# Block-diagonal keys against 64-row products in the attention scores of one stage of a four-layer kernel

## The chip, the cores and the metric

The kernel runs on one NeuronCore of a Trainium2 chip. The metric is the device time of one execution in microseconds (us). The times shown are medians of several executions, and a profile is one further execution taken by the hardware profiler.

## What is computed

The reference is a residual stack over x of shape 2 x 1024 x 256: in each of four layers a cross-attention block and a feed-forward block, each on the layer-normed x. The change lies in the feed-forward block of layer 0, here called L0 ffn, which is itself a small transformer: two layers of windowed local attention with a gated feed-forward. Cut to what matters:

```python
for l in range(2):                       # DEPTH
    q, k, v = split(shift_token(x) @ wqkv[l])      # 8 heads of 64
    q, k = rotary_xpos(l2norm(q) * qs, l2norm(k) * ksc)
    # windows of 128 queries, each on its own and the preceding window: 256 keys
    sim = einsum('bhwid,bhwjd->bhwij', bq * 8.0, bk)
    attn = softmax(where(mask, -big, sim))
    x = x + (attn @ bv) @ wo[l]
    h = layernorm(shift_token(x)) * g + b
    x = x + gated_gelu(h @ w1 + b1) @ w2 + b2
```

A head has 64 dimensions, so a score of one head is a product over 64 rows of the array of TensorE, which has 128 rows. Everything here is float32, apart from the mask, which is added to the scores as a bfloat16 product with the identity.

## The kernel before, in words

`l0_ffn` works through 32 items: two layers, eight tiles of 128 positions and two batches; four items (two tiles, two batches) make one turn of a hardware loop (`layers`, L896 and on). An item has its number `q` in the turn, its batch `b` (which picks one of two halves of the PSUM, banks 0 to 3 or 4 to 7), and `odd`, which says in which half of the key window its own keys stand. The work is a software pipeline written out by hand: `step(now, new, after)` is run on each engine, and in one step `now` goes from its probabilities to its output, `new` from its projections to its probabilities, and `after` has its input transposed. Each engine runs its list in order and waits for semaphores of the others. There is no planner.

TensorE's list in a step, in order: half of a projection of `new` (L977), `mixed(now)` (L1015, probabilities times values), projections of `new` between `mix_transposed` (L1023), `attention_out` (L1029) and `shifted` (L1035, L1036) of `now`, `h2_transposed` (L1042), `ffn_up` (L1052), `qk_transposed(new)` (L987), `y_transposed(after)` (L968), `ffn_down` of the first four of six chunks (L1061), then **scores(new)** (L998 and L999), the transposes of the probabilities of bank 0 (L1006), the last two chunks of `ffn_down` (L1061; the very last chunk has only 42 rows), and the transposes of banks 1 to 3 (L1006).

In `scores` one PSUM bank holds the scores of two heads, 2 x 256 columns. For each of four banks TensorE adds the mask (one product of 512 bfloat16 columns, L998) and then multiplies the 128 rows of queries of two heads by 128 rows of keys (512 columns, L999). So that two heads don't mix, the keys are block-diagonal: `kT` has for each pair of heads the keys of the one in rows 0 to 63 of the first 256 columns, those of the other in rows 64 to 127 of the last 256, and zeros elsewhere, which GpSimd writes once at the start (L839). A float32 product is carried out in two passes, so each of these is two MATMUL records with a load of weights (LDWEIGHTS) before each.

Around it: ScalarE copies the queries (`copy_qT`, L1140), VectorE the keys in two copies of 64 partitions (`copy_kT`, L1276). VectorE then takes, for each bank as it gets ready, the maximum of each row and head (`maxima`, L1286) and the bias of the exponential (L1287). ScalarE computes the exponentials of eight heads with their sums (`probs`, L1146), two per bank, as each bias gets ready. TensorE transposes the probabilities bank by bank (L1006); ScalarE copies banks 0 and 1 of the transposes (L1155) and VectorE banks 2 and 3 (`copy_pT`, L1293), and `mixed` waits for both. `mix` (L1297, L1300) divides by the sums.

Of the kernel before, what the change touches and what calls it, by code (L numbers as in the profile page):

```python
# [7 lines left out]
ALU = mybir.AluOpType  # L8
# [7 lines left out]
P = 128  # L16
BATCH, SEQ, D = 2, 1024, 256
# [48 lines left out]
def memory(e, ctx, stage):  # L66

    return lambda name, shape, dt=F32: ctx.enter_context(e.nc.sbuf_tensor(f"{stage}_{name}", shape, dt))


def flat(ap):
    return ap.rearrange("p a b -> p (a b)")
# [99 lines left out]
def build(nc, dram, out):  # L172
    with ExitStack() as ctx:
# [36 lines left out]
        with ExitStack() as early:  # L210
            ffn = L0Ffn(e, early)
            with ExitStack() as earlier:
                x1 = L0Xattn(e, earlier)
                prologue(e, x1)
                l0_xattn(e, x1, ffn)
            l0_ffn(e, ffn)
# [558 lines left out]
HEADS, DH = 8, 64  # L775
# [6 lines left out]
HALF = TILES // 2  # L782


def l0_ffn(e, ffn):

    nc, s, d, ps = e.nc, e.s, e.dram, e.psum
    dve, act, pool = (e.chain[n] for n in ("dve", "act", "pool"))  # L790
    with ExitStack() as ctx:
        sb = memory(e, ctx, "l0_ffn")
# [6 lines left out]
        mask_even = sb("mask_even", [P, HALF, 2 * P], BF16)  # L799
        mask_odd = sb("mask_odd", [P, 2 * P], BF16)  # L800
# [5 lines left out]
        pT = sb("pT", [P, BATCH, 2 * HEADS, P])  # L806
        ss = sb("ss", [P, BATCH, 2 * HEADS])
        rn = sb("rn", [P, BATCH, 2 * HEADS])
        qT = sb("qT", [P, BATCH, 4, P])
        kT = sb("kT", [P, BATCH, 4, 2, 2, P])  # L810
        vv = sb("vv", [P, BATCH, 2, INNER])
        top = sb("att_top", [P, BATCH, HEADS])
        scale = sb("att_scale", [P, BATCH, HEADS])
        bias = sb("att_bias", [P, BATCH, HEADS])
        den = sb("att_den", [P, BATCH, HEADS])
        rden = sb("att_rden", [P, BATCH, HEADS])
        o = sb("o", [P, BATCH, INNER])
        oT = sb("oT", [P, BATCH, 4, P])
        y1 = sb("y1", [P, BATCH, 2, D])
# [88 lines left out]
        with nc.Block() as block:  # L908
# [52 lines left out]
            def _(pe):  # L961
# [29 lines left out]
                def scores(m):  # L991
                    pe.wait_ge(s.v_ready.sem, s.v_ready.at(m.turn, m.k))
                    pe.wait_ge(s.qT_ready.sem, s.qT_ready.at(m.turn, m.k))
                    pe.wait_ge(s.kT_ready.sem, s.kT_ready.at(m.turn, m.k))
                    for j in range(4):
                        bank = ps[:, m.bank + j, :]
                        mask = (mask_odd[:].unsqueeze(1) if m.odd else mask_even[:, bass.ds(m.i, 1), :]).broadcast_to((P, 2, 2 * P))
                        pe.matmul(bank, e.ident_bf[:], mask, start=True, stop=False)  # L998
                        pe.matmul(bank, qT[:, m.b, j, :], kT[:, m.b, j, :, :, :].rearrange("p h w n -> p (h w n)"),  # L999
                                  start=False, stop=True).then_inc(s.scores_psum.sem, 1)  # L1000

                def probs_transposed(m, banks):
                    for j in banks:
# [6 lines left out]
                def mixed(m):  # L1010
                    pe.wait_ge(s.pT_act.sem, s.pT_act.at(m.turn, 2 * m.k))
                    pe.wait_ge(s.pT_dve.sem, s.pT_dve.at(m.turn, 2 * m.k))
                    for h in range(HEADS):
                        for c in range(2):
                            mm = pe.matmul(ps[:, m.bank, h * DH:(h + 1) * DH], pT[:, m.b, 2 * h + c, :],  # L1015
                                           vv[:, m.b, c, h * DH:(h + 1) * DH], start=(h, c) == (0, 0), stop=c == 1,
                                           skip_group_check=True)
                    mm.then_inc(s.mixed_psum.sem, 1)
# [48 lines left out]
                def first(new, after):  # L1067
                    y_transposed(new)
                    for n in range(3):
                        qkv(new, n)  # L1070
                    qk_transposed(new)
                    y_transposed(after)
                    scores(new)
                    probs_transposed(new, range(4))

                def step(now, new, after):
                    if new:
                        qkv(new, 0, (0,))
                    mixed(now)
                    if new:  # L1080
                        qkv(new, 0, (1,))
                    mix_transposed(now)
                    if new:
                        qkv(new, 1, (0,))
                    attention_out(now)
                    if new:
                        qkv(new, 1, (1,))
                    shifted(now)
                    if new:
                        qkv(new, 2)  # L1090
                    h2_transposed(now)
                    ffn_up(now)
                    if new:
                        qk_transposed(new)
                    if after:
                        y_transposed(after)
                    ffn_down(now, 0)
                    ffn_down(now, 1)
                    if new:
                        scores(new)  # L1100
                        probs_transposed(new, (0,))
                    ffn_down(now, 2)
                    if new:
                        probs_transposed(new, (1, 2, 3))
# [109 lines left out]
            def _(v):  # L1214
# [56 lines left out]
                def copy_kT(m):  # L1271
                    v.wait_ge(s.qkT_psum.sem, s.qkT_psum.at(m.turn, m.k))
                    v.wait_ge(s.scores_psum.sem, s.scores_psum.at(m.turn, 4 * (m.k - 2)))
                    for n in range(2):
                        own = slice(n * DH, (n + 1) * DH)
                        cp = v.tensor_copy(kT[own, m.b, :, n, m.odd, :], ps[own, m.bank + 1, :].rearrange("p (j n) -> p j n", j=4))  # L1276
                    cp.then_inc(s.kT_ready.sem, 1)

                def maxima(m):
                    v.wait_ge(s.q_norm_ready.sem, s.q_norm_ready.at(m.turn, m.k))  # L1280
                    v.wait_ge(s.probs_ready.sem, s.probs_ready.at(m.turn, 4 * (m.k - 2)))
                    v.tensor_scalar(scale[:, m.b, :], rn[:, m.b, 0:HEADS], float(DH) ** 0.5, None, ALU.mult)
                    for j in range(4):
                        v.wait_ge(s.scores_psum.sem, s.scores_psum.at(m.turn, 4 * (m.k - 1) + j + 1))
                        heads = slice(2 * j, 2 * j + 2)
                        dve.link(v.tensor_reduce(top[:, m.b, heads], ps[:, m.bank + j, :].rearrange("p (n x) -> p n x", n=2), AX.X, ALU.max))  # L1286
                        v.scalar_tensor_tensor(bias[:, m.b, heads], top[:, m.b, heads], -1.0, scale[:, m.b, heads],  # L1287
                                               ALU.mult, ALU.mult).then_inc(s.bias_ready.sem, 1)
# [5 lines left out]

                def mix(m):
                    v.wait_ge(s.probs_ready.sem, s.probs_ready.at(m.turn, 4 * m.k))
                    dve.link(v.reciprocal(rden[:, m.b, :], den[:, m.b, :]))  # L1297
                    v.wait_ge(s.mixed_psum.sem, s.mixed_psum.at(m.turn, m.k))
                    v.wait_ge(s.mixT_psum.sem, s.mixT_psum.at(m.turn, m.k - 2))
                    v.tensor_tensor(o[:, m.b, :].rearrange("p (h x) -> p h x", x=DH), ps[:, m.bank, :].rearrange("p (h x) -> p h x", x=DH),  # L1300
                                    rden[:, m.b, :].unsqueeze(2).broadcast_to((P, HEADS, DH)), ALU.mult).then_inc(s.mix_ready.sem, 1)

                def add_attention(m):
                    v.wait_ge(s.out_psum.sem, s.out_psum.at(m.turn, m.k))
# [45 lines left out]
                def first(new, after):  # L1350
                    take_y(new)
                    take_y(after)
                    tables(new.layer)
                    norms(new)
                    rotate_cos(new)
                    rotate_sin(new)
                    rotate_sum(new)
                    scale_k(new)
                    copy_kT(new)
                    maxima(new)  # L1360
# [1622 lines left out]
```

## Time and profile before

| what | value |
|---|---|
| median of 3 executions | 2155.83 us (2154.03 to 2156.53) |
| span of the profiled execution | 2156.2 us |
| TensorE matmuls busy | 1694.4 us (79%) |
| VectorE busy | 1111.4 us (52%) |
| ScalarE busy | 758.4 us (35%) |
| GpSimd busy | 438.6 us (20%) |
| L0 ffn, from its first scores to its last | 199.6 to about 1145 us of the span |

The profiled execution is one execution and its own time is its span, from its first to its last instruction. Shares are averages over stages that differ much: what a change in L0 ffn is worth is read from the stretch 199.6 to 1145 us alone. In the rows PE is a matmul, PEld a load of weights, DVE VectorE, ACT ScalarE, POOL GpSimd, and L followed by a number is the line of the kernel. The record of a matmul is longer than the time for which it keeps the next one waiting: starts are read from the records, ends are modelled.

### The profile page before, as it was taken

The numbers are of one execution on the slowest core, as the hardware profiler recorded it, in microseconds if no ns is written. First come the engines' busy times: TensorE is split into PE (matmuls) and PEld (weight loads), VectorE is DVE, ScalarE is ACT, GpSimd is POOL, SyncE is SP. The second block draws the span as 40 slices with busy tenths as digits, with TensorE's granted clock in tenths as the row PEclk, the third lists the DMA queues.
The fourth block names the chain that finished last, engine by engine and source line by source line (L and its number), as shares of the span: only waits on it lengthen the run. The fifth ranks groups of instructions, "written<-read, shape, count | busy, mean of one in ns | idle before, by whom it ended". The sixth has DMA issues, their size and how long they took to land. (4 is left out here: it accounts for less than half of the span.)

```text
span 2156.2 us, 31922 instructions
## 1 busy us (share of the span) xinstructions
PE 1694.4 (79%) x9560; PEld 1268.2 (59%) x9561; DVE 1111.4 (52%) x2565; ACT 758.4 (35%) x1808; POOL 438.6 (20%) x451
## 2 busy tenths in 40 slices
PE   5965999999999999999997839629824479847990
PEld 4653666666666666666666629528713147636990
DVE  3335555556555655565554650157666856562212
ACT  1211544445444444444443213204426223312330
POOL 1012111111111221222211122241131500007005
PEclk9977999999999999999997559869957589958995
DMA  5001000000001000000000212151000000014114
GB/s 199 0 0 46 1 1 0 0 0 0 0 1 46 1 1 0 0 0 0 0 1 29 88 63 66 56 195 56 3 27 0 0 3 0 0 40 115 34 36 122
DMA packets 30065, 66.49 MB, mean 31 GB/s; under 512 B 6438, under 2 KB 21815, under 8 KB 28460
## 3 DMA queue, kind: packets, MB, share of 16 engines
q1 hardware_dynamic: 23900, 48.99, 6.3%
q0 software_dynamic: 6096, 16.65, 2.9%
q8 instruction: 34, 0.56, 0.1%
q14 instruction: 35, 0.29, 0.0%
HBM read 51.04 MB, written 14.59 MB: 30 GB/s over the span
## 5 line engine op out<-in xcount | busy, mean ns | idle before, releaser
L1052 PE MATMUL banks<-l_ffn_h2T,l_ffn_w 128*128 128x128 f32 (+1 forms) x1536 | 185.0, 279 | 32.2 <-ACT l_ffn_h2T L1166 32.2
L1052 PEld LDWEIGHTS banks<-l_ffn_h2T,l_ffn_w 128*128 128x128 f32 (+1 forms) x1536 | 173.8, 182 | 42.9 <-issue 39.0
L977 PE MATMUL banks<-l_ffn_in_wqkv,l_ffn_hT 128*128 128x512 f32 x384 | 197.2, 611 | 1.9 <-issue 1.1
L1146 ACT ACTIVATE l_ffn_work<-banks,l_ffn_att_bias,l_ffn_att_scale 128x256 f32<-128x256 f32 x256 | 140.6, 568 | 51.8 <-DVE l_ffn_att_bias L1287 51.8
L942 POOL TENSOR_TENSOR l_ffn_rstd<-l_ffn_ve,neg_half 128x1 f32<-128x1 f32 x32 | 17.8, 557 | 658.2 <-DVE l_ffn_ve L1315 658.2
L1015 PEld LDWEIGHTS banks<-l_ffn_vv,l_ffn_pT 128*128 128x128 f32 x1024 | 119.3, 195 | 33.3 <-ACT l_ffn_pT L1155 29.6
L999 PE MATMUL banks<-l_ffn_kT,l_ffn_qT 128*128 128x512 f32 x256 | 132.8, 601 | 0.0
L1015 PE MATMUL banks<-l_ffn_vv,l_ffn_pT 128*128 128x64 f32 x1024 | 122.7, 279 | 8.8 <-DVE l_ffn_pT L1293 5.1
L1286 DVE TENSOR_REDUCE l_ffn_att_top<-banks 128x2 f32<-128x512 f32 x128 | 88.5, 692 | 62.3 <-PE banks L999 62.3
L256 POOL TENSOR_TENSOR rstd<-mean_var,neg_half 128x1 f32 (+1 forms) x80 | 46.0, 576 | 346.9 <-DVE mean_var L249 346.7
L1176 ACT ACTIVATE l_ffn_gate<-banks,l_ffn_layer_cols 128x128 f32<-128x128 f32 x192 | 59.8, 362 | 136.5 <-PE banks L1052 136.5
L2035 POOL DMA_INDIRECT l_experts_rows<-l_experts_y_rows,l_experts_back x64 | 62.4, 975 | 211.7 <-DMA l_experts_y_rows<-l_experts_y 192.8
L1061 PE MATMUL banks<-l_ffn_in_w,l_ffn_ff 128*128 128x256 f32 (+1 forms) x384 | 99.6, 388 | 0.0
L1160 ACT COPY l_ffn_oT<-banks 128x512 f32<-128x512 f32 x32 | 18.8, 586 | 202.1 <-PE banks L1023 202.1
L1300 DVE TENSOR_TENSOR l_ffn_o<-banks,l_ffn_att_rden 128x512 f32<-128x512 f32 x32 | 22.1, 692 | 130.6 <-PE banks L1015 99.6
L1899 POOL DMA_INDIRECT l_experts_rows<-l_experts_c_rows,l_experts_token x63 | 62.0, 984 | 128.3 <-POOLq L1795 109.7
L1183 ACT ACT_TABLE_LOAD x63 | 80.8, 1283 | 1.1
L1995 DVE COPY l_route_c_all<-l_ffn_in_w 128x1024 f32 x39 | 27.6, 709 | 103.4 <-PE banks L1928 90.7
L1928 PEld LDWEIGHTS banks<-l_experts_rowT,l_route_c_all 128*128 128x128 f32 x624 | 78.1, 197 | 1.9
L977 PEld LDWEIGHTS banks<-l_ffn_in_wqkv,l_ffn_hT 128*128 128x128 f32 x384 | 64.7, 195 | 24.0 <-issue 21.2
L1928 PE MATMUL banks<-l_experts_rowT,l_route_c_all 128*128 128x128 f32 x624 | 78.3, 281 | 0.0
L932 POOL TENSOR_TENSOR l_ffn_rn<-l_ffn_ss,neg_half 128x8 f32<-128x8 f32 x32 | 52.7, 1646 | 118.5 <-DVE l_ffn_ss L1247 118.5
(377 smaller groups left out, 3700.8 us busy)
## 6 DMA issues: line engine op xcount, KB each, us to landing
l_ffn_in_w<-in_L_w SPq DMA_DIRECT2D x2, 4096.0 KB, 20.2
l_experts_y_rows<-l_experts_y SPq DMA_DIRECT2D x63, 128.0 KB, 1.7
l_ffn_in_down<-in_L_down SPq DMA_DIRECT2D x1, 4096.0 KB, 13.0
l_experts_c_rows<-l_route_c_all SPq DMA_DIRECT2D x2, 2048.0 KB, 8.5
l_ffn_in_wqkv<-in_L_wqkv SPq DMA_DIRECT2D x1, 3072.0 KB, 12.8
l_ffn_w<-in_L_w SPq DMA_DIRECT2D x2, 1364.0 KB, 7.0
x_res<-in_x SPq DMA_DIRECT2D x4, 512.0 KB, 5.5
l_ffn_rot<-in_rotary SPq DMA_DIRECT2D x2, 1024.0 KB, 4.8
```

Of the source, the lines that this page charges most:

```text
L977: mm = pe.matmul(ps[:, m.bank + 1 + n, :], hT[:, m.b, m.odd, ch, 1 - ch:P + 1 - ch], wqkv[:, bass.ds(m.layer, 1), ch, n * INNER:(n + 1) * ...
L999: pe.matmul(bank, qT[:, m.b, j, :], kT[:, m.b, j, :, :, :].rearrange("p h w n -> p (h w n)"), start=False, stop=True).then_inc(s.scores_ps ...
L1015: mm = pe.matmul(ps[:, m.bank, h * DH:(h + 1) * DH], pT[:, m.b, 2 * h + c, :], vv[:, m.b, c, h * DH:(h + 1) * DH], start=(h, c) == (0, 0), ...
L1052: mm = pe.matmul(ps[0:FW[j], m.bank + j // 2, to:to + P], w1[:, ch, at:at + FW[j]], h2T[:, ch, m.b, :], start=(j % 2, n, ch) == (0, 0, 0), ...
L1061: mm = pe.matmul(ps[:, m.bank + 3, 0:D], ff[0:FW[j], j, :], w2[0:FW[j], bass.ds(m.layer, 1), j, :].rearrange("p l n -> p (l n)"), start=j ...
L1146: ex = nc.scalar.activation(work[:, m.b, slot, :], ps[:, m.bank + slot // 2, (slot % 2) * 2 * P:(slot % 2 + 1) * 2 * P], ACT.Exp, bias=bia ...
L1176: g = nc.scalar.activation(gate[0:FW[j], j, :], ps[0:FW[j], m.bank + j // 2, of:of + P], ACT.Gelu, bias=cols[0:FW[j], col:col + 1])
L1183: act.link(nc.scalar.activation(unused[:], zero, func))
L1286: dve.link(v.tensor_reduce(top[:, m.b, heads], ps[:, m.bank + j, :].rearrange("p (n x) -> p n x", n=2), AX.X, ALU.max))
L1899: p.indirect_dma_start(rows[:, t, :], None, c_rows, bass.IndirectOffsetOnAxis(ap=token[:, t:t + 1], axis=0))\
L1928: mm = pe.matmul(ps[m.j][:, f * P:(f + 1) * P], w, rowT[:, m.j, ch, :], start=(f, ch) == (0, 0), stop=ch == DCH - 1, skip_group_check=True)
L2035: p.indirect_dma_start(rows[:, i, :], None, y_rows, bass.IndirectOffsetOnAxis(ap=back[:, i:i + 1], axis=0))\
```

## The change

The keys are stored densely (`kT` has half the size, one copy of 128 partitions instead of two of 64), and each head becomes a product over 64 rows: heads with even numbers in rows 0 to 63, odd ones in rows 64 to 127, 256 columns each. Two heads that follow each other in the list use different row halves and write different banks. So that this is so, the order of heads in the banks changes (`slot_of`): a group `g` of four heads is held in two banks, bank `2g` with the two heads of the lower row half, bank `2g+1` with the two of the upper. In each group TensorE first adds the masks to both banks, and then issues four products: lower, upper, lower, upper. Banks `2g` and `2g+1` are both signalled near the end of their group. `scale`, the reciprocal of the sums and the products of `mixed` read and write in the changed order.

```diff
+def slot_of(head):
+    return head // 4 * 4 + head % 2 * 2 + head // 2 % 2
+def in_slots(ap):
+    return ap.rearrange("p (g n a) -> p g a n", g=2, n=2)
+def in_heads(ap):
+    return ap.rearrange("p (g a n) -> p g a n", g=2, n=2)
...
-        kT = sb("kT", [P, BATCH, 4, 2, 2, P])
+        kT = sb("kT", [P, BATCH, 4, 2, P])
...
-                    for j in range(4):
-                        bank = ps[:, m.bank + j, :]
-                        mask = (...)
-                        pe.matmul(bank, e.ident_bf[:], mask, start=True, stop=False)
-                        pe.matmul(bank, qT[:, m.b, j, :], kT[:, m.b, j, :, :, :].rearrange("p h w n -> p (h w n)"),
-                                  start=False, stop=True).then_inc(s.scores_psum.sem, 1)
+                    mask = (...)
+                    for g in range(2):
+                        for n in range(2):
+                            pe.matmul(ps[:, m.bank + 2 * g + n, :], e.ident_bf[:], mask, start=True, stop=True)
+                        for half in range(2):
+                            for n in range(2):
+                                own, j = slice(n * DH, (n + 1) * DH), 2 * g + half
+                                mm = pe.matmul(ps[:, m.bank + 2 * g + n, half * 2 * P:(half + 1) * 2 * P], qT[own, m.b, j, :],
+                                               flat(kT[own, m.b, j, :, :]), start=False, stop=True, skip_group_check=True)
+                                if half == 1:
+                                    mm.then_inc(s.scores_psum.sem, 1)
...
-                            mm = pe.matmul(ps[:, m.bank, h * DH:(h + 1) * DH], pT[:, m.b, 2 * h + c, :],
+                            mm = pe.matmul(ps[:, m.bank, h * DH:(h + 1) * DH], pT[:, m.b, 2 * slot_of(h) + c, :],
...
-                    for n in range(2):
-                        own = slice(n * DH, (n + 1) * DH)
-                        cp = v.tensor_copy(kT[own, m.b, :, n, m.odd, :], ps[own, m.bank + 1, :].rearrange("p (j n) -> p j n", j=4))
-                    cp.then_inc(s.kT_ready.sem, 1)
+                    v.tensor_copy(kT[:, m.b, :, m.odd, :], ps[:, m.bank + 1, :].rearrange("p (j n) -> p j n", j=4))\
+                     .then_inc(s.kT_ready.sem, 1)
...
-                    v.tensor_scalar(scale[:, m.b, :], rn[:, m.b, 0:HEADS], float(DH) ** 0.5, None, ALU.mult)
+                    v.tensor_scalar(in_slots(scale[:, m.b, :]), in_heads(rn[:, m.b, 0:HEADS]), float(DH) ** 0.5, None, ALU.mult)
...
-                    dve.link(v.reciprocal(rden[:, m.b, :], den[:, m.b, :]))
+                    dve.link(v.reciprocal(in_heads(rden_h[:, m.b, :]), in_slots(den[:, m.b, :])))
```

## Rows read from the trace of the kernel before

**Rows 1.** Two stretches: length, busy us of PE, PEld, DVE, ACT, POOL, granted clock, DMA.

```profile
199.50:681.00 481.50, 455.04 (x2554) 321.56 (x2555) 275.28 (x597) 225.38 (x578) 81.75 (x64) 0.99 0.01 3
...
719.00:1141.00 422.00, 396.84 (x2238) 281.01 (x2237) 249.59 (x573) 198.43 (x503) 89.12 (x84) 1.00 0.00 0
```

**Rows 2.** Timeline of TensorE over one step (start, us, instructions, idle before).

```profile
746.67 1.89 PE L1061 MATMUL banks<-l_ffn_in_w,l_ffn_ff 128*128 128x256 f32 x8
748.40 0.38 PE L998 MATMUL banks<-l_ffn_mask_odd,ident_bf 128*128 128x512 bf16 x1
748.62 1.02 PE L999 MATMUL banks<-l_ffn_kT,l_ffn_qT 128*128 128x512 f32 x2
...
752.70 0.60 PE L1006 MATMUL banks<-ident,l_ffn_work 128*128 128x128 f32 x4
...
754.29 1.56 PE L1006 MATMUL banks<-ident,l_ffn_work 128*128 128x128 f32 x12
755.69 1.02 PE L977 MATMUL banks<-l_ffn_in_wqkv,l_ffn_hT 128*128 128x512 f32 x2
756.85 3.76 PE L1015 MATMUL banks<-l_ffn_vv,l_ffn_pT 128*128 128x64 f32 x32
...
768.42 0.44 PE L1042 MATMUL banks<-ident,l_ffn_h 128*128 128x128 f32 x2 [0.45 <-DVE l_ffn_h L1321]
```

**Rows 3.** Timeline of VectorE in the same step.

```profile
749.68 0.69 DVE L1286 TENSOR_REDUCE l_ffn_att_top<-banks 128x2 f32<-128x512 f32 x1 [1.29 <-PE banks L999]
...
755.42 1.29 DVE L1293 COPY l_ffn_pT<-banks 128x512 f32<-128x512 f32 x2 [0.47 <-PE banks L1006]
```

**Rows 4.** Timeline of ScalarE in the same step.

```profile
750.66 0.56 ACT L1146 ACTIVATE l_ffn_work<-banks,l_ffn_att_bias,l_ffn_att_scale 128x256 f32<-128x256 f32 x1 [1.49 <-DVE l_ffn_att_bias L1287]
...
751.76 0.56 ACT L1146 ACTIVATE l_ffn_work<-banks,l_ffn_att_bias,l_ffn_att_scale 128x256 f32<-128x256 f32 x1
...
754.92 0.22 ACT L1146 ACTIVATION_READ_ACCUMULATOR l_ffn_work<-banks,l_ffn_att_bias,l_ffn_att_scale 128x1 f32 x1
```

**Rows 5.** Timeline from 128-row to 42-row chunks of L1061, in short windows.

```profile
753.14 0.60 PE L1061 MATMUL banks<-l_ffn_in_w,l_ffn_ff 128*128 128x256 f32 x2
...
753.66 0.70 PE L1061 MATMUL banks<-l_ffn_in_w,l_ffn_ff 42*128 42x256 f32 x2
...
754.29 0.20 PEld L1006 LDWEIGHTS banks<-ident,l_ffn_work 128*128 128x128 f32 x2 [0.33 <-ACT l_ffn_work L1146]
```

**Rows 6.** Timeline of two 64-row products in different row halves, L535, in growing windows.

```profile
63.71 0.48 PE L535 MATMUL banks<-ctx_tok,l_xattn_aT 64*128 64x256 f32 x1
...
63.71 0.49 PE L535 MATMUL banks<-ctx_tok,l_xattn_aT 64*128 64x256 f32 x2
...
63.71 0.70 PE L535 MATMUL banks<-ctx_tok,l_xattn_aT 64*128 64x256 f32 x4
```

**Rows 7.** Groups of VectorE's PSUM copies by form (count, busy us, mean ns, idle before).

```profile
L1276 DVE COPY l_ffn_kT<-banks 64x512 f32<-64x512 f32 x64 | 43.7, 683 | 2.5 <-PE banks L987 2.1
L1293 DVE COPY l_ffn_pT<-banks 128x512 f32<-128x512 f32 x64 | 41.2, 686 | 16.5 <-PE banks L1006 14.5 <-issue 1.3 <-DVE l_ffn_y L1227 0.7
```

**Rows 8.** Timelines at other steps: first, layer change, two behind a loop's branch.

```profile
199.55 0.59 PE L998 MATMUL banks<-l_ffn_mask_even,ident_bf 128*128 128x512 bf16 x1 [1.15 <-DVE l_ffn_kT L1276]
...
690.95 1.07 ACT L1155 COPY l_ffn_pT<-banks 128x512 f32<-128x512 f32 x2 [0.61 <-ACT l_ffn_layer_b L1115]
...
718.45 0.39 PE L998 MATMUL banks<-l_ffn_mask_even,ident_bf 128*128 x1
...
720.65 0.56 ACT L1146 ACTIVATE l_ffn_work<-banks,l_ffn_att_bias,l_ffn_att_scale 128x256 f32<-128x256 f32 x1 [1.55 <-DVE l_ffn_att_bias L1287]
...
814.45 0.42 DVE L1338 TENSOR_TENSOR x_res<-banks,l_ffn_y1b 128x256 f32 x1 [0.70 <-PE banks L1061]
...
816.52 1.29 DVE L1293 COPY l_ffn_pT<-banks 128x512 f32<-128x512 f32 x2 [0.54 <-issue]
```

**Rows 9.** Timeline of GpSimd and VectorE in the preparation of the stage.

```profile
169.46 3.51 POOL L839 MEMSET l_ffn_kT<- 128x4096 f32 x1 [0.31 <-POOLq L741]
172.91 1.95 POOL L840 MEMSET l_ffn_vv<- 128x2048 f32 x1
...
169.50 10.02 DVE L845 TENSOR_SCALAR l_ffn_y<-x_res,mean_var,rstd 128x256 f32<-128x256 f32 x16 [1.18 <-PEq L741]
```

More of the change, by code:

```diff
@@ L815, in l0_ffn @@
         den = sb("att_den", [P, BATCH, HEADS])
-        rden = sb("att_rden", [P, BATCH, HEADS])
+        rden_h = sb("att_rden", [P, BATCH, HEADS])
         o = sb("o", [P, BATCH, INNER])
@@ L994, in scores @@
                     pe.wait_ge(s.kT_ready.sem, s.kT_ready.at(m.turn, m.k))
-                    for j in range(4):
-                        bank = ps[:, m.bank + j, :]
-                        mask = (mask_odd[:].unsqueeze(1) if m.odd else mask_even[:, bass.ds(m.i, 1), :]).broadcast_to((P, 2, 2 * P))
-                        pe.matmul(bank, e.ident_bf[:], mask, start=True, stop=False)
-                        pe.matmul(bank, qT[:, m.b, j, :], kT[:, m.b, j, :, :, :].rearrange("p h w n -> p (h w n)"),
-                                  start=False, stop=True).then_inc(s.scores_psum.sem, 1)
+                    mask = (mask_odd[:].unsqueeze(1) if m.odd else mask_even[:, bass.ds(m.i, 1), :]).broadcast_to((P, 2, 2 * P))
+                    for g in range(2):
[8 more added lines that the diff above has]
+                                    mm.then_inc(s.scores_psum.sem, 1)
                 def probs_transposed(m, banks):
@@ L1300, in mix @@
                     v.tensor_tensor(o[:, m.b, :].rearrange("p (h x) -> p h x", x=DH), ps[:, m.bank, :].rearrange("p (h x) -> p h x", x=DH),
-                                    rden[:, m.b, :].unsqueeze(2).broadcast_to((P, HEADS, DH)), ALU.mult).then_inc(s.mix_ready.sem, 1)
+                                    rden_h[:, m.b, :].unsqueeze(2).broadcast_to((P, HEADS, DH)), ALU.mult).then_inc(s.mix_ready.sem, 1)
                 def add_attention(m):
```

## The prediction

> **What bounds the kernel now.** I read the busy times by stretch first. In L0 ffn TensorE's matmul records cover 852 of 903.5 us at a granted clock of 0.99 to 1.00, the 2.4 GHz level, and no other engine covers 60% [rows 1]. That looks like a stage in which every matmul saved is time saved. But records overlap, so I read one step's timeline next, TensorE first and then the engines that it meets around the scores.
>
> The step's scores start at 748.40 and the next work of TensorE, the transposes, at 752.70: 4.30 us for four banks, each a mask of 0.22 us and a product of two passes of 0.43 us (748.40 to 748.62, then 1.02 less the 0.59 of a record) [rows 2]. Next to it runs a second chain: bank 0 ready, VectorE's maximum at 749.68 (1.28 after the start of the scores), ScalarE's first exponential at 750.66, its last sum at 755.14, the last transposes, VectorE's second copy, and `mixed` at 756.85 [rows 2 to 4]. The eight exponentials go at 1.10 us for two (750.66 to 751.76) without a gap; they take 4.48 us in all [rows 4]. **Both chains arrive together.** TensorE's own work puts bank 3's transposes at about 755.2, and the last exponentials allow them at that time too; their record ends at 755.85 [rows 2]. VectorE copies two banks from 755.42, 1.29 us of which the second starts at 756.03 (1.29 less the 0.68 of one copy, [rows 3, 7]). So the second copy would bear bank 3 some 0.13 us later than it comes (756.03, against 755.85 and the 0.05 from a record's end to VectorE's start). After `mixed` all of TensorE's work follows in order, and what it waits for there (0.45 us at L1042, [rows 2]) hangs on `mixed` itself. **A step is therefore longer or shorter by what `mixed` moves against the start of the scores.**
>
> **The change, part by part.**
>
> *TensorE's work in the scores.* A group is now two masks (2 x 0.215 = 0.43), then 64-row products, 256 columns each. A pass of 256 float32 columns takes 0.215 us (0.60 less 0.38 for two of L1061) [rows 5]. Two 64-row products in different row halves run at once: L535 has four passes; the first alone has a record of 0.48 us, the first of both end 0.49 after the start, and all four are over in 0.70, where four passes in a row would need 0.48 + 3 x 0.215 = 1.1 [rows 6]. So a group's eight passes take four times 0.215 = 0.86. The price is the change of rows in use. After a 128-row pass that starts at 753.36 and streams to 753.57, the 42-row ones start at 753.66, and the second of them at 753.98 (753.66 + 0.70 - 0.38), so the first streams from 753.77: **0.20 us** in which nothing streams [rows 5]. Going back costs some 0.14 (0.09 to the load of weights at 754.29, and part of the load). A group: 0.43 + 0.20 + 0.86 + 0.14 = 1.63, a step's scores 3.26 instead of 4.30, 1.04 us less for TensorE.
>
> The Trainium skill, "TensorEngine Tiling (Array Packing)", section Theoretical Speedup, gives up to 2x for a contraction of 64 rows or fewer. By that figure alone the products' 3.42 us a step would halve, and 32 steps would save about 55 us; the trace agrees with the doubling in a pair, and against the rest stand the 0.34 us a group for the switches.
>
> *When the banks get ready.* Bank 0 was complete 0.22 + 0.86 = 1.08 after the start. Now it needs both masks, the switch and both of its heads: 0.43 + 0.20 + 0.86 = 1.49. **It is 0.41 us later**, while banks 1 to 3 are earlier (bank 1 1.49 for 2.15, bank 2 3.1 for 3.2, bank 3 3.1 for 4.3). VectorE needs about 0.89 us a bank, ScalarE 1.10, so only bank 0 sets the pace of the exponentials, and they all end 0.41 later: 755.55 for 755.14. Bank 3's transposes follow them; TensorE has nothing else to issue in between. Bank 3 is ready at 755.85 + 0.41 + 0.05 = 756.31, and VectorE, free at 756.03, waits 0.28. `mixed` is 0.28 us later. TensorE's gained 1.04 us is spent in waits before the transposes. In 9 of these steps, those behind a loop's branch, the exponentials start 2.20 after the scores (718.45 to 720.65, [rows 8]) and not 2.26, and it is 0.22. **27 like steps x 0.26 = +7.0 us.**
>
> *The steps that differ.* At the layer change ScalarE itself is last before `mixed` (its own copies follow the exponentials directly) [rows 8]: +0.4. At three ends of a turn in the second layer VectorE's copies come late, 816.52, behind statistics that wait for `ffn_down`, 814.45 [rows 8]. That product follows bank 0's transposes, which wait for two exponentials: 750.66 + 0.41 + 1.10 + 0.2 = 752.3 instead of 752.70. So it is 0.37 earlier: 3 x 0.37 = **-1.1**. In the first step the scores do wait for the keys' copy, 1.15 us [rows 8]: one copy of 128 partitions takes 0.69 like L1293's, for 1.37 with two [rows 7]: **-0.7**. I take its slower banks (half clock) as even, since its exponentials had gaps to fill.
>
> *The keys' copy elsewhere* frees 0.69 us of VectorE a step, 22 us in all, and I cost it at nothing: TensorE starts the scores 0.22 after the last pass of its own `ffn_down` (746.67 + 1.89 - 0.38 = 748.18, [rows 2]), at once, and VectorE then waits 1.29 us for bank 0 [rows 3]. If the copy were on the path it would give up to 0.1 a step.
>
> *The zeros.* GpSimd writes 4096 columns in 3.51 us, and VectorE's sixteen operations of that stretch stand still under it; the stage starts when they are done. 2048 columns take 1.95 [rows 9]: **-1.6**. The reordered views of 8 elements and the changed index in `mixed` change no count or size: nothing.
>
> **Sum:** 7.0 + 0.4 - 1.1 - 0.7 - 1.6 = **+4.0 us** on the profiled 2156.2, whose span is 0.4 above the median of 2155.83: 2159.8, or +0.18%. About 0.2%, 4.3 us, is what a measurement of this kernel can tell from no change.
>
> **Bounds of the unknown term**, the switch to 64 rows right behind a bfloat16 mask, which no row shows. With no cost, bank 0 is 0.21 late and the slack takes most of it: 27 x 0.06 + 0.2 - 3.4 = -1.6, 2154.2. At twice 0.20, a load and a gap not overlapping, 0.61 late: 27 x 0.46 + 0.6 - 0.9 - 2.3 = +9.8, 2165.6. I take 0.20, the nearest row.
>
> **Rivals.**
>
> *The products don't run together (slower).* Rows 6 show two products behind a wait; here four follow without one, and the load for the third could hold up the fourth. If the passes go one by one, bank 0 needs 0.43 + 0.20 + 6 x 0.215 = 1.92, 0.84 late, and a group costs TensorE 2.48, 4.96 a step for 4.30. `mixed` is 0.70 later in 27 steps: +18.9 + 0.8 + 2.0 (three ends) - 2.3 = +19.4, **2175**. It decides from the third pass on: bank 0 over 1.6 us after the start. Chance 9%. That two heads gain nothing at all from the halves is the same case: the change then doesn't do what it says.
>
> *TensorE's saving comes through (faster).* If `mixed` follows TensorE's list and not the exponentials, a step loses 1.04 us: 32 x 1.04 + 2.3 = 35.6, **2120**. For it speaks the full TensorE of rows 1. Against it: TensorE has only the transposes, two chunks and half a projection between scores and `mixed`, and the exponentials' 4.48 us can't start before bank 0. The skill, same page, section PSUM Bottleneck, says that tiling speeds up TensorE but not the reading of PSUM; the trace agrees, with 4.48 us of exponentials beside 3.26 of scores. Chance 9%.
>
> *The longer waits lower the clock.* TensorE would idle about 1.3 us a step more, in pieces under 0.6. With waits of such size the stretch holds 1.00 [rows 1, 2]. A few us, chance 4%.
>
> **Numbers.** The forecast with its bounds has 78%: of it 3% of all is faster by over 0.2%, 43% within, 32% slower. With the rivals: faster 12%, same 44%, slower 44%. The range is 2153.5 to 2166, the bounds with the runs' spread; the two rivals lie outside.
>
> **What would show it.** Pairs of L999 starts 0.01 apart, four starts 0.215 apart, behind a gap of 0.1 and a record longer by 0.1 (concurrency, switch). The first maximum 1.69 after the first mask for 1.28. ScalarE's exponentials still gapless. Waits of TensorE's loads in L1006 on ScalarE, new, some 1 us a step. `mixed` 8.7 us after the first mask for 8.45. GpSimd's first write at 1.95. A `mixed` less than 8.3 after the first mask would prove the forecast wrong, a first maximum after 1.9 the serial rival right.

## The result and the profile after

The changed kernel takes 2175.3 us (median of 4, 2174.60 to 2175.83), against 2155.18 for the kernel before (4 executions): a ratio of 1.0095, interval 1.0081 to 1.0109. It is 20 us slower, where the forecast had it 4 us slower and the range ended at 2166. The number 2175 stood in the prediction beside the serial rival. That is a coincidence: the trace shows another cause.

The page of the profile of the changed kernel: its span, busy times, granted clock by slices and the two queues that bring instructions:

```profile
span 2173.8 us, 32402 instructions
## 1 busy us (share of the span) xinstructions
PE 1678.0 (77%) x9816; PEld 1266.6 (58%) x9817; DVE 1080.3 (50%) x2533; ACT 757.5 (35%) x1808; POOL 436.0 (20%) x451
...
PEclk9977999999999999999998559959958579958995
...
q8 instruction: 35, 0.57, 0.1%
q14 instruction: 45, 0.37, 0.1%
```

TensorE is busy 16 us less than before and VectorE 31 us less, and the span is 17.6 us longer. The queue q14 carries 45 packets; it carried 35 in the kernel before.

TensorE in the step that answers to [rows 2] (start, us, instructions, idle before):

```profile
747.67 1.89 PE L1079 MATMUL banks<-l_ffn_in_w,l_ffn_ff 128*128 128x256 f32 x8
749.40 0.59 PE L1011 MATMUL banks<-l_ffn_mask_odd,ident_bf 128*128 128x512 bf16 x2
749.92 1.14 PE L1015 MATMUL banks<-l_ffn_kT,l_ffn_qT 64*128 64x256 f32 x8
750.99 0.61 PE L1011 MATMUL banks<-l_ffn_mask_odd,ident_bf 128*128 128x512 bf16 x2
751.52 1.13 PE L1015 MATMUL banks<-l_ffn_kT,l_ffn_qT 64*128 64x256 f32 x8
753.32 0.65 PE L1024 MATMUL banks<-ident,l_ffn_work 128*128 128x128 f32 x4 [0.66 <-ACT l_ffn_work L1164]
...
756.60 0.66 PE L1024 MATMUL banks<-ident,l_ffn_work 128*128 128x128 f32 x4 [0.44 <-ACT l_ffn_work L1164]
...
758.13 3.76 PE L1033 MATMUL banks<-l_ffn_vv,l_ffn_pT 128*128 128x64 f32 x32
```

The same place in two shorter windows, of which the first ends after one product's record and the second after two:

```profile
749.61 0.38 PE L1011 MATMUL banks<-l_ffn_mask_odd,ident_bf 128*128 128x512 bf16 x1
749.92 0.48 PE L1015 MATMUL banks<-l_ffn_kT,l_ffn_qT 64*128 64x256 f32 x1
...
749.92 0.49 PE L1015 MATMUL banks<-l_ffn_kT,l_ffn_qT 64*128 64x256 f32 x2
```

Here the forecast holds nearly to the hundredth. Two passes of a group are over in 0.49 us and all eight in 1.14, which is 0.49 and three more times 0.215: they run two at a time. A group repeats after 750.99 - 749.40 = 1.59 (forecast 1.63). New waits on ScalarE, 0.66 and 0.44 us, stand before the transposes, and `mixed` starts 8.73 after the first mask (forecast 8.7, before 8.45, [rows 2]).

VectorE and ScalarE in the same step, for [rows 3, 4]:

```profile
751.09 0.69 DVE L1302 TENSOR_REDUCE l_ffn_att_top<-banks 128x2 f32<-128x512 f32 x1 [2.54 <-PE banks L1015]
...
757.29 0.69 DVE L1309 COPY l_ffn_pT<-banks 128x512 f32<-128x512 f32 x1 [0.40 <-PE banks L1024]
```

```profile
752.07 0.56 ACT L1164 ACTIVATE l_ffn_work<-banks,l_ffn_att_bias,l_ffn_att_scale 128x256 f32<-128x256 f32 x1 [1.90 <-DVE l_ffn_att_bias L1303]
```

The first maximum is 1.69 after the first mask, as forecast, where it was 1.28. The like steps cost what was forecast for them. **Most of the time went elsewhere, at the ends of the turns in the second layer.** This is the end of the first of them, which answers to 814.45 and 816.52 in [rows 8], first on VectorE and then on TensorE:

```profile
815.57 0.42 DVE L1354 TENSOR_TENSOR x_res<-banks,l_ffn_y1b 128x256 f32 x1 [0.66 <-PE banks L1079]
...
816.95 0.16 DVE L1364 TENSOR_TENSOR mean_var<-mv,zero_eps 128x2 f32 x1
820.22 1.29 DVE L1309 COPY l_ffn_pT<-banks 128x512 f32<-128x512 f32 x2 [3.11 <-issue]
```

```profile
817.69 1.12 PE L990 MATMUL banks<-l_ffn_in_wqkv,l_ffn_hT 128*128 128x512 f32 x2
821.65 5.39 PE L1033 MATMUL banks<-l_ffn_vv,l_ffn_pT 128*128 128x64 f32 x32 [2.84 <-DVE l_ffn_pT L1309]
```

VectorE waits 3.11 us for nothing that the profile knows ("issue"), where it waited 0.54 [rows 8]. That is the place at which its loop goes back to its start. TensorE waits 2.84 us for VectorE, and then 32 passes take 5.39 us in place of 3.76. The busy times around it (start and end, length, PE, PEld, DVE, ACT, POOL, granted clock, DMA):

```profile
815.00:823.50 8.50, 5.19 (x33) 3.47 (x32) 2.65 (x8) 2.91 (x10) 0.56 (x1) 1.00 0.01 4
823.50:830.30 6.80, 6.80 (x25) 5.15 (x24) 0.69 (x1) 0.48 (x1) 0.00 (x0) 0.50 0.00 0
830.30:846.00 15.70, 14.20 (x87) 11.06 (x86) 10.33 (x23) 7.19 (x17) 5.80 (x5) 1.00 0.00 0
```

From 823.5 on the granted clock is 0.50, the 1.2 GHz level, for 6.8 us. The same stands at the second turn's end, with waits of 3.04 and 2.72 us. The last turn's end is another matter: VectorE has no such wait there, but the clock fell to 0.50 too, from about 1076 to 1083, behind waits of TensorE of 0.60, 0.44 and 0.79 us.

### The profile page after: what moved, and what is told of

It reads as the page before. It is cut to its first block and busy times, and to the rows that moved or that the text cites. A ratio compares the mean times of both kernels' runs of the same rounds, so it can differ in the third digit from the quotient of the medians.

```text
span 2173.8 us, 32402 instructions
## 1 busy us (share of the span) xinstructions
PE 1678.0 (77%) x9816; PEld 1266.6 (58%) x9817; DVE 1080.3 (50%) x2533; ACT 757.5 (35%) x1808; POOL 436.0 (20%) x451
## 5 line engine op out<-in xcount | busy, mean ns | idle before, releaser
L1033 PEld LDWEIGHTS banks<-l_ffn_vv,l_ffn_pT 128*128 128x128 f32 x1024 | 125.7, 204 | 32.8 <-ACT l_ffn_pT L1173 25.1
L1033 PE MATMUL banks<-l_ffn_vv,l_ffn_pT 128*128 128x64 f32 x1024 | 129.1, 288 | 8.7 <-DVE l_ffn_pT L1309 6.4
L1024 PE MATMUL banks<-ident,l_ffn_work 128*128 128x128 f32 x512 | 80.2, 287 | 34.9 <-ACT l_ffn_work L1164 34.9
L1079 PE MATMUL banks<-l_ffn_in_w,l_ffn_ff 128*128 128x256 f32 (+1 forms) x384 | 99.6, 388 | 0.0
L1024 PEld LDWEIGHTS banks<-ident,l_ffn_work 128*128 128x128 f32 x512 | 53.7, 141 | 69.8 <-ACT l_ffn_work L1164 55.3
```

Source lines behind the costliest of these rows:

```text
L1024: mm = pe.transpose(ps[:, m.bank + j, n * P:(n + 1) * P], work[:, m.b, 2 * j + n // 2, (n % 2) * P:(n % 2 + 1) * P], e.ident[:])
L1079: mm = pe.matmul(ps[:, m.bank + 3, 0:D], ff[0:FW[j], j, :], w2[0:FW[j], bass.ds(m.layer, 1), j, :].rearrange("p l n -> p (l n)"), start=j ...
```

## The experiments

Two theories. **A, placement:** the change removes one VectorE instruction of each step's list (the second copy of the keys), nine of them ahead of the second layer's loop. All later code of VectorE moves forward by nine instructions and the loop's body shrinks from 278 to 274. It now lies so that its return has to wait for instructions from memory. **B, the scores:** TensorE's new waits bring the clock down, and the long turns are a consequence. The experiments ran in two sets on two chips, on both of which the kernel before is slower than in the result; the second set is the change again, the heads in another order, and the scores moved in the kernel before. The kernel before takes 2206.85 us (21 executions) with the first set and 2208.49 (15) with the second, 2.4% more. Like steps of L0 ffn are as long on all of them to a few hundredths. From the last scores to the end it is 1061 to 1070 us there and 1015 in the trace of the kernel before, so the difference lies behind this stage. Ratios and differences are taken within a set unless it is said.

### Nine instructions put back

```diff
                     tables(new.layer)
+                    for n in range(9):
+                        v.memset(ff[:, 0, n:n + 1], 0.0)
```

> The changed kernel with nine one-column memsets put into VectorE's list once, where VectorE waits for the first squares, so that all its later code stands nine instructions further on, as before the change. Theory A (placement: the second layer's loop body of VectorE, 274 instructions, has come to lie over one more 8 KB piece of code, and its return waits 2.9 us for instructions): the branch's wait is back at about 0.3 us in each of the turns, the clock stays at 1.00 through the second layer, and the time is about 2160 (2158 to 2162), 15 us less than the change's 2175.3. Theory B (the scores: the new waits of TensorE before the transposes bring the clock down, and the long turns are its consequence): nothing moves, 2175. In both the first maximum stands 1.69 us after the first mask and mixed 8.73 after it.

2210.28 us (11 executions), ratio to the kernel before 1.0016 (1.0007 to 1.0025), which is 3.4 us more (1.5 to 5.5). The turn's end, the instruction queue, and the stretch of the second layer:

```profile
814.22 0.16 DVE L1364 TENSOR_TENSOR mean_var<-mv,zero_eps 128x2 f32 x1
814.92 1.29 DVE L1309 COPY l_ffn_pT<-banks 128x512 f32<-128x512 f32 x2 [0.54 <-issue]
```

```profile
q14 instruction: 35, 0.29, 0.0%
```

```profile
749.00:1140.00 391.00, 356.42 (x2167) 255.55 (x2166) 219.26 (x518) 182.90 (x466) 82.71 (x78) 1.00 0.00 0
```

The wait at the return is gone, ten packets of instructions are gone, and the clock is 1.00 throughout, with all of TensorE's new waits before the transposes still there. Theory B falls for the two returns. Nine writes of one column took away most of the loss, which the next run measures in these conditions. What is left, 3.4 us, agrees with the forecast's 4.0.

### The change again, in the second set

> The changed kernel itself, on the chip of the experiments, for a direct comparison with the nine memsets (3.4 us above the kernel before there). Theory A: some 14 to 17 us more than with them, about 17 to 20 us above the kernel before, ratio 1.008 to 1.009.

2223.43 us (5 executions), 1.0073 (1.0058 to 1.0088): 15 us above the kernel before. It is 13.0 above the run of the same set that has the nine writes and the heads in another order, and by the differences to the kernel before, 14.9 and 3.4, it is 11.5 above the nine writes alone: a little under what was expected. In this execution two turns' ends have the wait (3.00 in the row below) and half a clock behind it. The last turn's end has the same waits of TensorE as in the result (0.61, 0.44 and 0.78 us) and the full clock, and its step is 3.1 us shorter than there. So that part differs between executions of one kernel, and its cause stays open.

```profile
818.20 1.29 DVE L1309 COPY l_ffn_pT<-banks 128x512 f32<-128x512 f32 x2 [3.00 <-issue]
```

### The keys copied twice

```diff
-                    v.tensor_copy(kT[:, m.b, :, m.odd, :], ps[:, m.bank + 1, :].rearrange("p (j n) -> p j n", j=4))\
-                     .then_inc(s.kT_ready.sem, 1)
+                    for n in range(2):
+                        own = slice(n * DH, (n + 1) * DH)
+                        cp = v.tensor_copy(kT[own, m.b, :, m.odd, :], ps[own, m.bank + 1, :].rearrange("p (j n) -> p j n", j=4))
+                    cp.then_inc(s.kT_ready.sem, 1)
```

> The changed kernel with the keys copied in two copies of 64 partitions, as before, into the dense keys; the products are those of the change. VectorE's loop bodies then have as many instructions as before the change, 256 and 278, and stand where they stood. Theory A: no long wait at the return, about 2160.5 (0.7 us more than with the nine memsets, from the first step, where the copy is on the path). Theory B: 2175 or more, since TensorE's list is the change's. If the keys' copy were on the path in every step: 0.69 us x 31 = 21 us more than with the nine memsets.

2212.06 us (10 executions), 1.0034 (1.0019 to 1.0050). No long wait, 35 packets on q14: the placement is restored without any filler. It is 1.8 us above the nine writes where 0.7 was expected, and far from the 21 that the copy would cost on the path. The first mask of the stage:

```profile
195.92 1.01 PE L1011 MATMUL banks<-l_ffn_mask_even,ident_bf 128*128 128x512 bf16 x2 [1.15 <-DVE l_ffn_kT L1294]
```

It waits 1.15 us for the keys, where it waits 0.45 with the nine writes: the 0.70 of the first step, as forecast. The other steps, the layer change left aside, are together 1.35 us longer than with the nine writes, most of it at ends of turns, so the second copy accounts for about 2 us. The times themselves are less sharp than that: six executions lie between 2210.7 and 2212.2 and four between 2215.5 and 2222.3, for a reason that no trace here shows. In the profiled execution the layer change ran at the full clock and its step took 32.58 us for 37.09 with the nine writes, one more place where the clock differs between executions.

### The kernel before, moved by 115 instructions

```diff
                     tables(new.layer)
+                    for n in range(115):
+                        v.memset(ff[:, 0, n:n + 1], 0.0)
```

> The kernel before with 115 one-column memsets put into VectorE's list once, in its wait for the first squares (some 7 us of work in a wait of 6 us, so at most 2 us of cost by themselves). Theory A: its loop of the second layer, 278 instructions, starts 115 further on and lies over one more piece of 128 instructions: a wait of about 2.9 us at two returns, half a clock for about 7 us behind them, and 2155.2 + 12 to 16 = about 2169 (2165 to 2173). Theory B, or any in which the products matter: at most 2157.

2219.69 us, 1.0058 (1.0043 to 1.0073): 12.8 us slower, as theory A had it, with no change to any product or copy.

```profile
816.10 0.16 DVE L1348 TENSOR_TENSOR mean_var<-mv,zero_eps 128x2 f32 x1
819.41 1.29 DVE L1293 COPY l_ffn_pT<-banks 128x512 f32<-128x512 f32 x2 [3.15 <-issue]
```

```profile
q14 instruction: 46, 0.38, 0.1%
```

```profile
819.50:829.70 10.20, 8.85 (x35) 7.69 (x36) 2.00 (x4) 0.00 (x0) 0.00 (x0) 0.50 0.00 2
```

The steps at these two ends take 38.04 and 38.43 us for 31.29 and 31.30 in the kernel before, 13.9 more together, which accounts for the whole loss. Their waits of TensorE are longer than in the changed kernel (3.67 and 3.55 us), and so is the half clock behind them, 10.2 us for 6.8. Wait, packets and half clock are all made by place alone. The number 115 was chosen on the assumption that instructions are held in pieces of 128: a shift by 115 forward then puts the body where a shift by 13 backward would, close to the 9 backward of the change. It bore out, but other numbers were not tried, so the length of a piece is supported and not shown.

The Trainium skill, "Runtime: NRT & Kernel Launch", section Instruction fetch mechanics, says that an engine's instruction memory is filled in sequence and that a taken branch to a place outside it waits for a fetch; this case's traces agree on the branch, and give the price at a loop's return: 3.1 us for 0.54. The same section has blocks of 16 KiB; the packets of q14 here hold 8 KB each (0.37 MB in 45). Whether one or two of them make a block no run here shows directly. That 9 backward and 115 forward both bring the wait speaks for one, if 128 instructions fill a packet: the two places lie 124 instructions apart.

### Heads in another order

```diff
-                        for half in range(2):
-                            for n in range(2):
+                        for n in range(2):
+                            for half in range(2):
```

This run has the nine writes too.

> The changed kernel with the nine memsets, and with the products of a group in the order lower, lower, upper, upper in place of lower, upper, lower, upper. If the array takes products of the other row half only as they come up in the list, the two halves overlap in part or not at all: bank 1 gets ready up to 0.86 us later, a group costs TensorE 2.0 to 2.5 us for 1.6. Bank 0 is ready as before, 1.69 after the first mask with VectorE's start. By the forecast's mechanism partial overlap (groups of 2.0) costs nothing, since TensorE has 0.66 us of waits before the first transposes: as the nine memsets, within 3 us. With no overlap at all TensorE's list becomes the bound: mixed about 9.1 after the first mask, +0.4 us x 31 = 12 us.

2210.46 us (10 executions), 1.0007 (0.9997 to 1.0017): 2.0 us above the kernel before, as with the nine writes within the noise. The products did not lose their overlap at all:

```profile
748.58 0.49 PE L1015 MATMUL banks<-l_ffn_kT,l_ffn_qT 64*128 64x256 f32 x2
...
748.58 1.14 PE L1015 MATMUL banks<-l_ffn_kT,l_ffn_qT 64*128 64x256 f32 x8
749.65 0.60 PE L1011 MATMUL banks<-l_ffn_mask_odd,ident_bf 128*128 128x512 bf16 x2
```

Eight passes in 1.14 us again, though the first four in the list use the lower rows and the last four the upper. One after the other, the eight would need 0.48 + 7 x 0.215 = 2.0, and the first two, which are over in 0.49 (the first row, from a short window), would need 0.70. So in this list the products of the upper half did not wait for those of the lower half ahead of them. The serial rival and the partly serial one are both out.

### Scores ahead of a part of ffn_down

```diff
                     ffn_down(now, 0)
-                    ffn_down(now, 1)
                     if new:
                         scores(new)
+                    ffn_down(now, 1)
+                    if new:
                         probs_transposed(new, (0,))
```

This was run once in the changed kernel with the nine writes, and once in the kernel before.

> The changed kernel with the nine memsets, and with the scores of the next item moved ahead of the second pair of chunks of ffn_down (0.86 us of TensorE's work). By the forecast's mechanism (mixed hangs on bank 0, not on TensorE's list) the scores start up to 0.8 us earlier, which the keys' copy now allows (it ends 0.92 us before the first mask, in the kernel before 0.21), and the 0.86 us go into the wait before the transposes: about 0.75 us less in each of 31 steps, 2160 - 23 = about 2137 (2130 to 2143), faster than the kernel before. If TensorE's own list set the step, the order would change nothing: 2160.

In the changed kernel: 2191.72 us (4 executions, 2186.73 to 2195.49), ratio to the kernel before 0.9924 (0.9908 to 0.9939), 18.6 us less than with the nine writes (expected: 23) and **15 us less than the kernel before**. TensorE, where the first masks now follow four passes of L1079 and the other four stand behind the scores:

```profile
737.63 1.03 PE L1079 MATMUL banks<-l_ffn_in_w,l_ffn_ff 128*128 128x256 f32 x4
738.59 0.59 PE L1011 MATMUL banks<-l_ffn_mask_odd,ident_bf 128*128 128x512 bf16 x2
...
741.78 1.13 PE L1079 MATMUL banks<-l_ffn_in_w,l_ffn_ff 128*128 128x256 f32 x4
742.75 0.60 PE L1024 MATMUL banks<-ident,l_ffn_work 128*128 128x128 f32 x4
...
745.79 0.66 PE L1024 MATMUL banks<-ident,l_ffn_work 128*128 128x128 f32 x4 [0.36 <-ACT l_ffn_work L1165]
747.33 3.76 PE L1033 MATMUL banks<-l_ffn_vv,l_ffn_pT 128*128 128x64 f32 x32
```

The wait of 0.66 before the first transposes is filled, and `mixed` is again 8.74 after the first mask, though 0.86 us more of TensorE's work lies between them. A step is 29.46 us (738.59 to 768.05) for 30.23 (749.40 to 779.63): 0.77 less, as expected. From the first mask of the stage to the last the two profiled executions take 924.9 us and, with the nine writes, 946.6: 21.7 less. The first mask comes 5.0 later here (199.25 for 194.22): 3.4 of that stand before the first work of TensorE in this stage, in code that the move doesn't touch, and 1.6 come from a longer stretch at the slow clock in the first projections.

> The kernel before with the scores of the next item moved ahead of the second pair of chunks of ffn_down. There the copies of the keys end only 0.21 us before the first mask and TensorE has no waits in the scores' neighbourhood to fill, so that the move alone should bring little: the first mask can come at most 0.1 us earlier, and ffn_down's 0.86 us then stand in TensorE's way before the transposes: 0 to 0.1 us a step, within 4 us of the kernel before. If it gains as much as in the changed kernel (20 us against its base), the dense keys have no part in that gain.

In the kernel before the same move costs time: 2234.48 us (4 executions), 1.0123 (1.0105 to 1.0140), 26 us more. The expectation of at most 4 us was wrong.

```profile
758.90 1.03 PE L1061 MATMUL banks<-l_ffn_in_w,l_ffn_ff 128*128 128x256 f32 x4
760.56 0.38 PE L998 MATMUL banks<-l_ffn_mask_odd,ident_bf 128*128 128x512 bf16 x1 [0.63 <-DVE l_ffn_kT L1277]
...
764.85 1.03 PE L1061 MATMUL banks<-l_ffn_in_w,l_ffn_ff 128*128 128x256 f32 x4
...
769.87 3.76 PE L1015 MATMUL banks<-l_ffn_vv,l_ffn_pT 128*128 128x64 f32 x32 [0.18 <-DVE l_ffn_pT L1294]
```

The first mask waits 0.63 for the keys' second copy, and `mixed` comes 9.31 after it instead of 8.45: TensorE's list is full there, so the moved 0.86 us is paid in full after the scores, and with the wait before them almost nothing of it comes back: a step takes 30.75 us for 29.95. The expectation had named both and set them off against each other. By these rows the gain of the move needs both things that the dense keys bring, the shorter list of TensorE and the earlier copy; a kernel with only one of them was not run with the move.

## Why the prediction was wrong

- **The groups and the overlap: right.** 1.59 us a group for 1.63; two row halves at once, the switch to 64 rows at 0.20: the first pair starts at 749.92, 0.31 after the second mask, with the first record 0.1 longer, as in front of the 42-row chunk [rows 5].
- **Bank 0 late by 0.41, `mixed` by 0.28: right.** 0.41 and 0.28 were measured. Both chains arriving together, and TensorE's saved 1.04 us a step ending as waits, is what happened. The contrast of the two reordered kernels shows it from the other side.
- **First step and zeros: right in size.** The first mask comes 2.8 us earlier for a forecast of 2.3 (196.78 for 199.55, [rows 8]): its wait for the keys is 0.45 us for 1.15, and VectorE's sixteen operations of [rows 9] take 8.31 for 10.02.
- **The step that failed: "the steps that differ", the three ends of a turn at -0.37 each.** It took VectorE's way from `ffn_down` to its late copies as fixed apart from its start, and so it put the loop's return, which lies on that way, at no change. -1.1 us was forecast for the three. Measured against the kernel with the nine writes, two of them took 5.6 us more each (36.36 and 36.41 for 30.79 from mask to mask) and the third 3.1, in all 14.3. In the first two, the later `mixed` that VectorE's return brings makes 2.5 to 2.6 of it, and half a clock behind TensorE's wait the other 3.0 to 3.1. The 3.1 of the third are a half clock without such a wait, which the second run of the same kernel doesn't have; that the placement brings it is not shown. With the nine writes in place the first two ends are what was forecast: `mixed` 9.21 after the first mask, forecast 9.22.
- **The third end: wrong also by itself, by 0.6 us.** It was counted like the other two, but `mixed` waits for ScalarE there:

```profile
1073.43 4.70 PE L1033 MATMUL banks<-l_ffn_vv,l_ffn_pT 128*128 128x64 f32 x32 [0.79 <-ACT l_ffn_pT L1173]
```

```profile
1071.01 1.28 ACT L1173 ACT_TABLE_LOAD   x1
1072.30 1.07 ACT L1173 COPY l_ffn_pT<-banks 128x512 f32<-128x512 f32 x2
```

A load of a table stands between the exponentials, which end 0.41 later, and ScalarE's copies. In the kernel before the copies of the two engines ended there 0.05 apart (1059.82 ScalarE, 1059.87 VectorE). So `mixed` comes 9.53 after the first mask where it came 9.26, and not 0.37 earlier.

- **The keys' copy "costed at nothing": right for its time, wrong for its code.** The prediction counted what the removed instructions did and not where the ones behind them would lie. The forecast of +4.0 was measured at +3.4 and +2.0 in the two runs in which the placement is as before. These intervals reach from -0.7 to 5.5, so the size of the agreement is in part luck.
- **The rivals.** The serial one and TensorE's saving coming through are both refuted, the one by the passes in pairs and the other by `mixed`, which comes at 8.73 and not before 8.45. That waits lower the clock had 4%, on account of the waits before the transposes; in the like steps those leave it at 1.00. The clock did fall behind the waits of 2.7 to 2.8 us that the fetch makes, a cause that the prediction didn't list.

## What to carry to other kernels

Ask of a faster operation which chain it starts, not only how long it lasts: here the scores of a step need 1 us less of TensorE and deliver their first bank 0.4 us later, and only moving other work into the gap turns that into a gain. When instructions are removed or added, look at the loops behind them on the same engine: compare the packets of the instruction queues and the "issue" wait at each loop's return before any theory on the change itself. Nine idle instructions were worth some 12 us.

## What the runs showed of the hardware

- At two returns of a loop VectorE waited 3.00 to 3.15 us in each of three traces (the result, the change again, the kernel before moved by 115), and 0.54 in the kernel before and with the nine writes. Ten or eleven more packets on q14 go with it.
- Behind a wait of TensorE of 2.84 us the clock stood at 0.50 for 6.8 us, behind one of 3.67 for 10.2. Behind waits of 0.6, 0.4 and 0.8 us at one place it fell in one execution of the changed kernel and not in another.
- Float32 products on different row halves ran in pairs in both orders tried: 1.14 us for eight passes of 256 columns as lower, upper, lower, upper and as lower, lower, upper, upper.
- The same program took 2155 us in the result's runs and 2207 and 2208 on the chips of the experiments, while the steps in this stage agree to a few hundredths of a microsecond.
